# Six-layer gated recurrence on one core: two DMA transposes of layer 0 become TensorE transposes, with their rests a step earlier

## The reference, cut to what matters

```python
# state: (2048, 256) fp32; token: (2048,) int32; ih: (6, 4000, 256); hh: (6, 256, 256)
for i in range(6):
    gate = ih[i][token]
    state = tanh(state + matmul(state, hh[i]) * gate)
return state
```

## Time and profile before

| | before |
|---|---|
| runs | 96.0, 96.92, 97.68 us; median 96.92 |
| profiled execution | 97.14 us, of which the span of the profile is 95.3 |
| busy share of the span | PE 89%, DVE 83%, ACT 81%, POOL 72% |
| granted clock of PE | 0.989 of full speed over the span |
| chain that ended last | PE 51%, DVE 20%, DMA 15%, issue 6%, POOL 4% |

### The profile page before, as it was taken

One profiled execution on the slowest core, in us unless ns is written; L12 is line 12 of the kernel. 1 busy time (PEld: TensorE's weight loads), 2 busy tenths in 40 slices (PEclk: granted clock), 3 DMA queues, 4 the chain that ended last, 5 costly groups with the idle time before them and its releaser, 6 DMA issues.

```text
span 95.3 us, 1876 instructions
## 1 busy us (share of the span) xinstructions
PE 85.3 (89%) x688; PEld 76.1 (80%) x688; DVE 79.6 (83%) x128; ACT 76.8 (81%) x133; POOL 68.4 (72%) x63
## 2 busy tenths in 40 slices
PE   5957997999994988999999999999999999999900
PEld 5947885989873866998999999998999999988800
DVE  1239993969729799899998999989999999989980
ACT  5039999999974669998999989999899969975551
POOL 3487877877787089859988689877698589877000
PEclk9999999999999999999999999999999999999995
DMA  2899999852994905952545815556255515556984
GB/s 29 254 377 399 322 281 320 239 169 73 125 122 131 130 21 111 105 110 46 98 76 109 102 33 98 104 110 65 52 110 110 110 23 104 99 110 145 385 300 160
DMA packets 27224, 13.99 MB, mean 147 GB/s; under 512 B 23756, under 2 KB 24012, under 8 KB 27216
## 3 DMA queue, kind: packets, MB, share of 16 engines
q1 hardware_dynamic: 24720, 11.81, 56.1%
q0 software_dynamic: 2496, 2.07, 7.5%
HBM read 17.05 MB, written 2.10 MB: 201 GB/s over the span
## 4 chain that ended last, share of the span: by engine, by line
PE 51%; DVE 20%; DMA 15%; issue 6%; POOL 4%; ACT 0%; SPq 0%; POOLq 0%; DVEq 0%
PE products L298 43%; PE turned L330 7%; DVE gates L433 6%; DMA gates<-in_gate_rows,index 6%; DVE sums L471 5%; DMA last_rows<-in_gate_last 5%; POOL gates L275 4%; DVE sums L483 4%; DMA split_cols<-split_rows 4%; DVE split_rows L495 2%; DVE sums L468 1%; PE spare L339 1%; DVE split_cols L488 1%; ACT state L406 0%; PE spare L348 0%
## 5 line engine op out<-in xcount | busy, mean ns | idle before, releaser
L298 PE MATMUL products<-w_head,split_cols 128*128 128x256 f16 x316 | 55.0, 273 | 0.3 <-DMA split_cols<-split_rows 0.3
L282 POOL TENSOR_TENSOR sums<-sums,state 128x512 f32<-128x512 f32 x36 | 45.5, 1272 | 10.9 <-DVE sums L471 10.6
L298 PE MATMUL products<-w_rest,split_cols 128*128 128x256 f16 x158 | 43.1, 273 | 0.0
L406 ACT ACTIVATE state<-sums 128x512 f32<-128x512 f32 (+1 forms) x49 | 30.3, 619 | 10.7 <-DVE sums L483 5.1
L298 PEld LDWEIGHTS products<-w_head,split_cols 128*128 128x128 f16 x316 | 30.9, 98 | 4.0 <-DMA split_cols<-split_rows 0.6
L471 DVE SCALAR_TENSOR_TENSOR sums<-products,w_down,gates 128x512 f32<-128x512 f32 (+1 forms) x40 | 29.5, 737 | 2.2 <-PE products L298 2.2
L298 PEld LDWEIGHTS products<-w_rest,split_cols 128*128 128x128 f16 x158 | 15.5, 98 | 1.8
L290 PE MATMUL products<-w_full,first_cols 128*128 128x256 f32 x64 | 15.1, 381 | 1.6 <-DMA w_full<-in_weights 1.6
L275 POOL DMA_INDIRECT gates<-in_gate_rows,index x12 | 13.3, 1110 | 3.7 <-issue 3.4
L290 PEld LDWEIGHTS products<-w_full,first_cols 128*128 128x128 f32 x64 | 11.6, 190 | 3.0 <-issue 1.7
L370 ACT ACTIVATE gates<-last_rows 128x1536 f32<-128x1536 f32 (+1 forms) x8 | 10.6, 1390 | 4.2 <-DMA last_rows<-in_gate_last 4.2
(11 more groups left out here) (37 smaller groups left out, 46.9 us busy)
## 6 DMA issues: line engine op xcount, KB each, us to landing
first_cols<-in_state_cols SPq DMA_DIRECT2D x8, 256.0 KB, 4.5
out<-state SPq DMA_DIRECT2D x7, 256.0 KB, 2.4
w_full<-in_weights SPq DMA_DIRECT2D x6, 256.0 KB, 5.2
last_rows<-in_gate_last SPq DMA_DIRECT2D x1, 768.0 KB, 5.0
split_cols<-split_rows SPq DMA_TRANSPOSE x20, 3.1
out<-state SPq DMA_DIRECT2D x2, 128.0 KB, 1.7
gates<-in_gate_rows,index POOLq DMA_INDIRECT x12, 4.8
gates<-in_gate_first,index POOLq DMA_INDIRECT x4, 5.6
```

The costliest lines, as they stand in the source:

```text
L282: nc.gpsimd.tensor_tensor(sums[:, q], sums[:, q], pair_rows(state, q), ALU.add).then_inc(pool_added, 1)
L298: last = nc.tensor.matmul(bank[:, j, :], split_cols[:, q, s, j, k, :], w[:, l - 1, k * HID:(k + 1) * HID], start=(n == 0), stop=(n == len( ...
L406: nc.scalar.activation(pair_rows(state, q)[:, cut], sums[:, q, cut], ACT.Tanh).then_inc(state_ready, 1)
```

## The change

Pairs 1 and 3 of layer 0 are taken off the DMA way and put on PE's. And `make_rest` follows four steps after the product for the pairs of layer 0, five for all others, as before.

```diff
--- before.py
+++ after.py
@@ -34,11 +34,13 @@
 
 
     DMA_PAIRS = (1, 3, 5, 7)
-    PE_INSTEAD = ()
+    PE_INSTEAD = ((0, 1), (0, 3))
 
     TURN_LAG = 3
     HEAD_LAG, HEAD_ROWS_LAG = 3, 1
     REST_LAG, REST_ROWS_LAG = 5, 3
+
+    FIRST_REST_LAG = 4
 
 
     LAST_ON_DVE = (4, 5, 6, 7)
@@ -515,7 +517,9 @@
             for i in range(STEPS):
                 for n, cut in enumerate(cuts(i)):
                     gated(i, n, cut)
-                    if n == 0 and i >= REST_LAG and by_pe(i - REST_LAG):
+                    if n == 0 and FIRST_REST_LAG <= i < PAIRS + FIRST_REST_LAG and by_pe(i - FIRST_REST_LAG):
+                        make_rest(i - FIRST_REST_LAG)
+                    if n == 0 and i >= PAIRS + REST_LAG and by_pe(i - REST_LAG):
                         make_rest(i - REST_LAG)
                     if n == 0 and i >= REST_ROWS_LAG and by_dma(i - REST_ROWS_LAG):
                         make_rest_rows(i - REST_ROWS_LAG)
```

## The result

The changed kernel takes **98.17 us** in the median of 20 runs (97.02 to 101.5); the kernel before, run beside it 20 times, 96.7 (95.81 to 99.02). The ratio is **1.0123, 95% interval 1.0093 to 1.0153**: 1.2% slower, where the forecast was 96.8 us and no change that can be told.

What follows compares the result with a forecast made beforehand. PE bounds everything from p13 on, so only p13's start counts, set by single waits before it. Totals(1) -0.68, rest(4) +0.60, landing 0 to -0.19: -0.1 to -0.3 us, forecast 96.8 us, range 95.9 to 98.5.

Steps and rivals of the forecast that it cites:

- Step 1: Gather ahead of gated(6): without pair 1's transpose, tile 13 lands in 2.9 to 3.7 us, not 5.62; wait nearly goes.
- Step 2: PE in layer 0: two turns (0.88 us) and a 0.44 wait delay p8 by 1.32; totals(1) still 0.68 earlier.
- rival 1: Gated(6): the gather stays late regardless of the transpose, so p13 comes 1.47 us late, 98.4 us; 15%.
- the 2.2 us of full durations: PE's two turns: if eight transposes held PE fully, 2.2 us instead of 0.88, totals(1) 0.64 later, 98.1 us in all.
- Step 3: DVE after gated(8): rest(4) adds 0.60 us before the rows of pair 5, leaving 0.08 us of the gain.
- Step 4: Landing of pair 5's transpose: 3.71 us as before, p13 at 38.02; bounds 3.1 and 6.2 us.
- Rival 2: Pair 5's transpose: being first makes it slow, 6.2 us to land, p13 +2.4 us, 99.3 us; 7%.
- Step 5: Turn(10) waits for state through gated(9), POOL and ACT: no earlier than 39.15, capping the gain at about 0.27 us.
- Rival 3: Gather and transpose colliding makes runs differ; without it always the lower time, 96.0 us, a gain of 0.9; 15%.

Runs made afterwards that it cites:

- e1: The changed kernel run again, unedited, on an occasion with late layer 0: 105.75 us beside 102.57 for the kernel before.
- e2: The changed kernel with the rests of pairs 4 and 6 of layer 0 at five steps, late occasion: 103.94 us beside 102.57.
- f3: The kernel before with only the lag of four for layer 0's rests, no added turns, late occasion: 103.87 us, ratio 1.0171.
- e3: The kernel before with only the lag of four for layer 0's rests, no added turns, late occasion: 105.22 us beside 102.57.
- occasions e, f and h: Three occasions of follow-up runs with layer 0 late in every kernel profiled; the kernel before took 102.6, 103.4 and 104.2 us.
- h3: The changed kernel with all rests at five steps, so the turns alone, late occasion: 114.03 us, ratio 1.1241.

## Why the prediction was wrong, by its steps

From gated(8) to turn(10), and the span, in the profiles of the undisturbed occasions (us; "to SP" is the issue of pair 5's transpose):

| kernel | gated(8) | to SP | landing | turn(10) | span |
|---|---|---|---|---|---|
| before, two profiles | 32.98; 32.26 | 1.36; 1.38 | 3.71; 3.71 | 39.42; 38.71 | 95.3; 94.6 |
| changed | 32.72 | 1.96 | 4.01 | 40.06 | 96.0 |
| changed, rests 4, 6 at five | 32.79 | 1.37 | 3.97 | 39.50 | 95.4 |
| before, rows of pair 5 early | 33.27 | -0.78 | not waited for | 39.20 | 95.1 |

**Step 1 is the step that failed.** What it said would be seen was seen: gated(6) without a wait, 0.60 us behind add(5), though the gather took 4.1 us and not 2.9 to 3.7. But it took one late landing, 5.62 us, for the rule of this kernel, and counted its wait of 2.41 us as time to be won. In the second profile of before the same gather took 3.5 with the transpose beside it; gated(6) starts at 26.60 there and at 26.62 in the changed kernel.

With the wait goes the cover that Step 2 counted on. In the second profile fr7 starts at 28.97, when p8, from 27.66 on, is just over. PE stands still for 1.65 us there too, but elsewhere: 0.92 us ahead of fr5, 0.24 ahead of fr6 and 0.49 ahead of totals(1), which starts at 31.21. That is 0.11 earlier than the 31.32 that Step 2 forecast for the changed kernel. So even a forecast that came true to the last digit would have been a gain of 0.68 us against the first profile and a small loss against the second.

Five profiles bear on whether the transpose crowds the gathers (us to landing, tiles 13, 14 and 15 being the last gathers of layer 0):

| kernel | transpose of pair 1 issued at | tile 13 | tile 14 | tile 15 |
|---|---|---|---|---|
| before, first | 22.63 | 5.6 | 5.6 | 4.9 |
| before, second | 23.66 | 3.5 | 3.9 | 4.0 |
| before, rows of pair 5 early | 24.56 | 3.6 | 4.0 | 4.6 |
| changed | none | 4.1 | 3.6 | 3.7 |
| changed, rests 4, 6 at five | none | 3.7 | 3.2 | 3.4 |

Tiles 14 and 15 landed 0.3 us or more later in every profile with the transpose than in either without it; tile 13, issued ahead of it each time, was late only where the transpose followed 0.28 us behind. The crowding that Step 1 inferred is thus likely, though five executions of four programs don't isolate it; its size was what one execution had. The transpose itself took 6.2, 4.0 and 4.6 us in the first three, and 3.1 in the kernel before without gathers.

On the claim of the Trainium skill quoted with rival 1 ("Advanced Engine Details and Errata", X-Bar Transpose (TRN2): transposing DMAs as fast as regular ones), the page of the changed kernel has, with the median us to landing at the end:

```profile
out<-state SPq DMA_DIRECT2D x7, 256.0 KB, 2.4
...
split_cols<-split_rows SPq DMA_TRANSPOSE x18, 3.0
```

Each of these transposes moves the 256 KB of a head and a rest. So they are 0.6 us slower than a store of that size, and the trace does not quite bear the claim out (the two go to different places, which no run separates); but that is a surplus of its own, and no evidence of crowding. The 6.2 and 3.7 us that the prediction held against the claim were not compared with any regular DMA.

**Step 2: its prices held, its start didn't.** Four transposes back to back cost 0.44 us, in the chain after (25.91 to 26.35) and at both added turns without gathers; the 2.2 us of full durations, the alternative put beside the Trainium skill's 275 ns (which the page has for a bf16 tile; the turns here are fp32), did not come. But rest(0) stands behind gated(4), which waited for the gather of tile 9 and came 0.37 us later than I took it, from the first profile (21.68 for 21.31), and PE needed 0.12 more from the rest to the turn: turn(2) at 23.12 for 22.63. This ran through to p8 (28.79 for 28.27) and to totals(1) (31.84 for 31.32). In the second profile of before gated(4) comes at 22.34. I took a start that varies by 1 us as a number. With gathers the turns and their shorter lag cost 0.2% (1.0021), without them 1.2% (0.9803 to 0.9921): so gathers do give them cover, or are relieved by them; these runs don't separate the two.

**Step 3 held:** gated(8) to the rows of pair 5 took 1.26 us (forecast 1.26), and the transpose came 1.96 behind gated(8) for 1.96. That a step which costs 0.60 was set against a gain from one profile is what turned the sign.

**Step 4** was 0.30 us short: 4.01 for 3.71, inside its bounds. **Rival 2**, a first transpose that takes 6.2 us, fell: where the one that p13 waits for is the first of the program it took 4.01, 3.97, 3.89 and 3.88 (e1, e2), where it is the third 3.71, 3.71, 3.75 and 3.95 (f3, e3). Without gathers it is the other way round: 3.1 as the first, in both changed versions, and 3.68 as the third. So no cost of a first use is shown, and it is not the cause of 6.2; what sets the 0.3 us of Step 4 stays open.

**Step 5** named the right mechanism, but as a cap on a gain. It is also a way for rest(4) to cost: it moves gated(9), POOL's add and the state by 0.6 us even when the landing is quick, as without gathers.

In sum, profile against profile: forecast -0.14 us (97.0 for 97.14), measured +0.64 (97.78). Of the 0.78 between them 0.42 is gated(8) (32.72 for 32.30) and 0.30 the landing. The ratio says more than that, 1.2 us, since the profile of before was itself a late one: 97.14 us beside 96.42 in the second and 96.7 in the median of 20. Against the second profile the changed kernel has gated(8) 0.46 us later and 0.89 more from there to turn(10), together 1.35. **Rival 1** had come nearest in its outcome (98.4 us), for another reason: it let the gather stay late, and it did not. **Rival 3**'s time of 96.0 us did not come: the fastest of the changed kernel's twenty runs took 97.02. Its cause is not refuted, and not shown. Without a transpose in layer 0 the changed kernel's runs spread more (4.5 us, beside 3.2), those of the changed kernel with rests 4 and 6 at five less (1.05 us, beside 3.07).

## What to carry to other kernels

Where a stretch is bound by a wait for a DMA, profile the same program twice before a gain is counted from that wait: here the wait of 2.41 us was gone in the second profile, and two waits for other gathers stood in its place. An instruction moved ahead of the one that feeds a transfer, or a chain over three engines, costs its whole time at the end, however much of the engine is idle elsewhere: rest(4) cost 0.6 us in each of the pairs compared. And a shorter lag which one part of the loop needs should be given to that part alone.

## What the runs showed of the hardware

**PE's signal reaches DVE late, on some occasions.** In e1, DVE's add of step 5 waits 6.02 us. It needs fr5, which by PE's record was over at 26.31, while gathers were landing until 32.5. By the timeline of DVE, which says `remote` where the semaphore rose just before the start but no instruction is found that ended then:

```profile
24.63 0.69 DVE L485 TENSOR_TENSOR sums<-sums,spare 128x512 f32<-128x512 f32 x1 [1.26 <-remote]
...
33.20 0.69 DVE L485 TENSOR_TENSOR sums<-sums,spare 128x512 f32<-128x512 f32 x1 [6.02 <-remote]
```

In the profile of the result the same add waited 0.59 us and started at 26.02. Such waits, 1.3 to 7.3 us, are in eleven of the twelve profiles of the occasions e, f and h (not in h3), and in none of the others; the kernel before took 5.7 to 7.5 us longer there. That the gathers hold PE's signal up is only argued, and what brings it about stays open.

**The granted clock falls behind it.** The same execution, by the table of stretches (start:end, length, each engine busy, granted clock, DMA share, GB/s):

```profile
29.00:30.00 1.00, 0.69 (x4) 0.26 (x2) 0.00 (x0) 0.00 (x0) 0.97 (x1) 1.00 0.26 57
...
31.00:32.00 1.00, 0.00 (x0) 0.00 (x0) 0.00 (x0) 0.00 (x0) 0.27 (x1) 0.88 0.16 36
32.00:33.00 1.00, 0.00 (x0) 0.00 (x0) 0.00 (x0) 0.00 (x0) 0.00 (x0) 0.50 0.22 51
...
39.00:40.00 1.00, 1.00 (x12) 0.90 (x10) 0.66 (x1) 0.00 (x0) 0.00 (x0) 1.00 0.00 0
```

PE stood still from 29.7 us, and its clock went from 1.00 to 0.50, the lower of its two levels, 1.2 GHz; it was back at 1.00 from 39 us on. Four transposes for a turn take 1.09 us at the lower level (h3, above) and 0.60 at the upper. The idle ahead of turn(2) in the changed kernel, 0.95 us, did nothing of the kind: the granted clock is 1.00 in each us from 21 to 26 there, and 0.992 in the mean of its span (0.989 in the kernel before).
